# Attention and mixture of experts: early slots on GpSimd, late choices ahead of the shared units, and a reordered opening

## The chip, the cores and the metric

The kernel runs on one core of one Trainium2 chip. The metric is device time in microseconds (us), the median of several runs. The engines are called by their short names: PE is TensorE, DVE is VectorE, ACT is ScalarE, POOL is GpSimd, and SP is SyncE, which here only issues DMAs.

## What is computed

Two batches of 1024 tokens of width 256 go through causal attention with 16 query heads and 4 key-value heads of width 128, with rotary positions, then a layer norm, then a mixture of 64 experts, of which each token takes 6, with two shared units beside them, then a second layer norm. Cut to what matters:

```python
q = q * cos + _rotate_half(q) * sin;  k = k * cos + _rotate_half(k) * sin
attn = softmax(where(causal, q @ k.T * scale, min));  out = (attn @ v) @ Wo.T
x = _layernorm(x + out)
scores = softmax(x @ gate_w.T);  topk_w, topk_ids = top_k(scores, 6)
topk_w = topk_w / (sum(topk_w) + 1e-20)
act = silu(g) * u                       # g, u = x through w_gate_up of each expert, width 176
routed = sum over the 6 experts of topk_w * (act @ w_down.T)
x = _layernorm(x + routed + shared(x))  # shared: the same with ws_gate_up, ws_down, width 352
```

## The kernel before

Every float32 product of the attention and of the experts is made of three products of halves: a value is copied rounded (`..._hi`, on ACT) and the rest is kept (`..._lo`, on DVE or POOL), and PE sums hi*hi, hi*lo and lo*hi (lines 871 to 873).

**Attention** (`attention`, L253) is written as a pipeline over steps. A step scores 128 queries of one head against their keys. There are four rounds of 64 steps (k = 0 to 3), two rounds for each batch, with a part ahead of them (k = -1) that fills the pipeline. In every engine's program the body runs over n from 7 to 70, and each engine does at n what is due for step n, n - 1, n - 2 and so on, in the order in which the lines stand. Semaphores are counted in numbers known when the program is written. What else is due at a step is given by tables. `FILLS` (L82) gives the steps at which PE fills `proj_ps` with the projection of K, of V (T is V's projection, transposed by PE in the fill V), of Q or of the output O; the bank is single, so each fill waits until the one before is copied. `fill_at` (L212) looks the step up, and in the first part puts K at step 51 and T at step 55 by hand. Behind a fill of K or Q comes a turn (rotary position): ACT copies the bank to `taken` (L591), POOL multiplies the two halves of the partitions by the cosine (L528, L530), DVE multiplies by the sine (L784), POOL adds (L538), ACT copies to `q_hi` or `k_hi` (L618), and POOL makes `q_lo` or `k_lo` (L401), except for the first K and the first Q, where DVE does. In the rounds POOL's multiplication is one instruction (L534) for the last turns, and DVE's two (L786, L787).

The first batch's 1024 tokens are routed while the second batch is in attention. `EARLY_DVE` (L91) gives DVE's parts of this by (round, step): statistics, norms, the best 8 of 64 logits, their ids, a mask of the six chosen experts, the softmax weights, and 12 parts "slot" for each of two groups of 512 tokens (L765 to L773): for each of six choices, compare the ids, multiply by `slot_of`, sum over the 64 experts, and convert to an integer address. With such an address POOL sends the tokens' rows to the experts' areas in DRAM (`send`, L492; 48 sends by `EARLY_FILL`), once ACT has filled one of four row buffers. DVE waits behind each slot's operation for its end (`then`).

**The rest** (`feed_forward`, L1045) begins behind a barrier. The other 1024 tokens, in two groups g = 0, 1, are routed by DVE between the units of the shared experts: `tops`, `ids`, `choices`, `masks`, `weights`, `places` and `slot(g, j)`; `notes(g)` puts the weights into the rows, and then POOL may send the rows, 24 indirect DMAs a group (L1272). A shared unit is a gate-and-up product on PE (L1767), a SiLU on ACT (L1362), two products on DVE (`shared_hide`, L1487), a down product on PE (L1781) and an addition on DVE (`shared_add`). When all 48 sends have landed and the last shared unit is gated, SP loads the first expert block's rows (L1209), and a loop over blocks of 256 rows follows, with the expert's weights loaded as they come. At the end the results are summed, normed and stored.

Of the kernel before, what the change touches and what calls it, by code (L numbers as in the profile page):

```python
# [21 lines left out]
F32 = mybir.dt.float32  # L22
# [64 lines left out]
         "O": [4 * (i // 2) + 8 + i % 2 for i in range(2 * QUADS)]}  # L87
ROPES = sorted([("K", i) for i in range(2 * KV_ROUND)] + [("Q", i) for i in range(QUADS)],
# [20 lines left out]
             (2, 43): [(0, "slot", 0)], (2, 47): [(0, "slot", 1)], (2, 50): [(0, "slot", 2)],  # L109
             (2, 51): [(0, "slot", 3), (0, "slot", 4)], (2, 53): [(0, "slot", 5)], (2, 54): [(0, "slot", 6)],  # L110
             (2, 55): [(0, "slot", 7), (0, "slot", 8)], (2, 57): [(0, "slot", 9)], (2, 58): [(0, "slot", 10)],
             (2, 59): [(0, "slot", 11), (1, "norm", 0)], (2, 61): [(1, "norm", 1)], (2, 62): [(1, "norm", 2)],
# [3 lines left out]
             (3, 29): [(1, "weigh", 0)], (3, 30): [(1, "weigh", 1)], (3, 35): [(1, "slot", 0)],  # L116
             (3, 39): [(1, "slot", 1)], (3, 43): [(1, "slot", 2)], (3, 47): [(1, "slot", 3)],
             (3, 50): [(1, "slot", 4)], (3, 51): [(1, "slot", 5), (1, "slot", 6)], (3, 53): [(1, "slot", 7)],
             (3, 54): [(1, "slot", 8)], (3, 55): [(1, "slot", 9), (1, "slot", 10)], (3, 57): [(1, "slot", 11)],
             (3, 58): [(2, "stats", 0), (2, "stats", 1)], (3, 59): [(2, "stats", 2), (2, "stats", 3)],  # L120
             (3, 60): [(2, "moments", 0), (2, "moments", 1)], (3, 62): [(2, "inverse", 0)],
             (3, 63): [(2, "norm", 0), (2, "norm", 1)], (3, 64): [(2, "norm", 2)], (3, 65): [(2, "norm", 3)]}
# [5 lines left out]
BESIDE_COPIED = {(2, 17): (2, 1), (3, 17): (4, 2)}  # L128
RING_ROWS = 4
# [82 lines left out]
def fill_at(n, first):  # L212


    if first and n in (STEPS + FILLS["T"][0], STEPS + FILLS["K"][0]):
        return ("K" if n == STEPS + FILLS["T"][0] else "T"), len(FILLS["K"])
# [36 lines left out]
def attention(nc, dram, resid, consts):  # L253
    with ExitStack() as ctx:
# [34 lines left out]
        stats, moments = sb("early_stats", [P, NORMED, 6]), sb("early_moments", [P, NORMED, 2])  # L289
# [1676 lines left out]
```

## Time and profile before

| | us |
|---|---|
| median of 3 runs | 1334.73 |
| lowest, highest | 1334.47, 1335.14 |
| the profiled execution, whole | 1332.91 |
| its span, from the first instruction to the last | 1331.1 |

Of this span about 28 us are the opening, until the first scores; the four rounds reach to about 905 us; the late tokens' routing and the shared units reach to about 994; the expert loop and the closing take the rest. The profile gives times from the start of the span. A row of the timeline is: start, duration, engine, line of the kernel, operation, what it writes and reads, shapes, and in brackets the idle time of the engine ahead of it with what ended it. A row of instruction groups has, behind the count, the busy time in us and the mean of one in ns, and then the idle time ahead of them. A row of windows has the stretch, its length, the busy times of PE, of PE's weight loads, of DVE, ACT and POOL, each with its number of instructions, then the granted clock of PE as a share of full speed, the share of DMA time and GB/s.

### The profile page before, as it was taken

Reading aid. Unit: us, or ns where it says so; the run is one execution under the profiler, and the core shown is the slowest. Engines: PE = TensorE matmul, PEld = TensorE weight load, DVE = VectorE, ACT = ScalarE, POOL = GpSimd, SP = SyncE. Lnnn points to the kernel's source line nnn. Section 1 sums busy time; section 2 is a strip of 40 time slices with the busy share of each in tenths; the row PEclk is TensorE's granted clock in tenths of the full one; section 3 lists DMA queues with packets and bytes.
Section 4 is the critical chain, followed back from the end, with each engine's and each line's share of the span. In section 5 each row is a group of like instructions: output and inputs, shape, how many; then the busy total and the mean of one; then the engine's idle time right before and its main releaser. Section 6 shows DMA issues by size and latency. Waiting matters only on the chain. (4 is left out here: it accounts for less than half of the span.)

```text
span 1331.1 us, 28521 instructions
## 1 busy us (share of the span) xinstructions
PE 1227.7 (92%) x8636; PEld 1105.6 (83%) x8636; DVE 1023.2 (77%) x2162; ACT 859.0 (65%) x1973; POOL 790.4 (59%) x796
## 2 busy tenths in 40 slices
PE   5899999999999999989999998997969999999967
PEld 3799889889889889878888886886859999999955
DVE  2677777677677777878877887886837999999946
ACT  3665666666576666656666565676227999988932
POOL 5654744654584464365456445443775888888852
PEclk7999999999999999999999999998989999999979
DMA  7766765776558785676577567750357888888857
GB/s 249 204 184 164 187 184 154 186 201 172 147 127 209 212 212 141 164 191 171 162 185 205 136 174 204 187 139 20 95 168 218 259 266 260 255 267 262 263 217 309
DMA packets 196601, 256.51 MB, mean 193 GB/s; under 512 B 13642, under 2 KB 167678, under 8 KB 196500
## 3 DMA queue, kind: packets, MB, share of 16 engines
q1 hardware_dynamic: 183332, 227.85, 61.7%
q0 software_dynamic: 11040, 25.30, 5.7%
q10 hardware_dynamic: 2128, 2.10, 0.5%
q8 instruction: 54, 0.88, 0.3%
q14 instruction: 47, 0.39, 0.1%
HBM read 90.43 MB, written 169.72 MB: 195 GB/s over the span
## 5 line engine op out<-in xcount | busy, mean ns | idle before, releaser
L846 DVE TENSOR_REDUCE neg_max<-scores 128x1 f32<-128x256 f32 (+7 forms) x256 | 192.2, 751 | 152.1 <-PE scores L969 151.4
L608 ACT ACTIVATE pt_hi<-pt 128x512 fp32r<-128x512 f32 (+3 forms) x384 | 174.7, 490 | 188.1 <-PE pt L978 186.1
L581 ACT ACTIVATE probs<-scores,neg_max 128x256 f32<-128x256 f32 (+7 forms) x256 | 189.8, 742 | 48.4 <-DVE neg_max L846 48.3
L802 DVE TENSOR_TENSOR pt_lo<-pt,pt_hi 128x512 fp32r<-128x512 f32 (+3 forms) x384 | 200.3, 549 | 22.7 <-ACT pt_hi L608 21.0
L871 PE MATMUL o_ps<-pt_hi,v_hi 128*128 128x256 f32 (+1 forms) x640 | 193.7, 303 | 8.7 <-DVE o_lo L810 8.5
L872 PE MATMUL o_ps<-pt_lo,v_hi 128*128 128x256 f32 (+1 forms) x640 | 180.0, 281 | 0.0
L873 PE MATMUL o_ps<-pt_hi,v_lo 128*128 128x256 f32 (+1 forms) x640 | 179.6, 281 | 0.0
L978 PE MATMUL pt<-ident,probs 128*128 128x128 f32 x1152 | 169.6, 274 | 6.2 <-DVE pt_lo L802 6.2
L538 POOL TENSOR_TENSOR turned<-turned,turn_sin 128x512 f32<-128x512 f32 x80 | 105.5, 1318 | 114.5 <-DVE turn_sin L784 59.3
L1291 POOL DMA_INDIRECT results_dram<-rows,dest x134 | 145.1, 1083 | 33.1 <-issue 26.4
L969 PE MATMUL scores<-k_hi,q_lo 128*128 128x512 f32 (+4 forms) x384 | 151.8, 395 | 0.0
L528 POOL TENSOR_TENSOR turned<-taken,cos 64x512 f32<-64x512 f32 x60 | 79.5, 1325 | 112.7 <-ACT taken L591 100.2
L978 PEld LDWEIGHTS pt<-ident,probs 128*128 128x128 f32 x1152 | 135.1, 141 | 13.2 <-issue 5.8
L401 POOL TENSOR_TENSOR q_lo<-turned,q_hi 128x512 fp32r<-128x512 f32 x63 | 81.3, 1291 | 101.9 <-ACT q_hi L618 101.3
L964 PE MATMUL scores<-k_hi,q_hi 128*128 128x512 f32 (+4 forms) x384 | 133.2, 347 | 1.6 <-DVE q_lo L401 1.4
L871 PEld LDWEIGHTS o_ps<-pt_hi,v_hi 128*128 128x128 f32 x640 | 121.5, 190 | 14.5 <-issue 7.7
L965 PE MATMUL scores<-k_lo,q_hi 128*128 128x512 f32 (+4 forms) x384 | 131.3, 342 | 0.0
L872 PEld LDWEIGHTS o_ps<-pt_lo,v_hi 128*128 128x128 f32 x640 | 122.2, 191 | 0.0
L873 PEld LDWEIGHTS o_ps<-pt_hi,v_lo 128*128 128x128 f32 x640 | 121.5, 190 | 0.0
L830 DVE SCALAR_TENSOR_TENSOR resid<-proj_ps,row_inv,resid 128x256 f32<-128x256 f32 x256 | 110.0, 470 | 5.9 <-PE proj_ps L873 5.8
L871 PE MATMUL proj_ps<-wo_hi,o_hi 128*128 128x256 f32 x256 | 78.3, 306 | 21.1 <-DVE resid L830 10.4
L871 PE MATMUL proj_ps<-x_hi,w_hi 128*128 128x512 f32 x192 | 79.6, 414 | 15.0 <-DVE w_lo L383 8.0
(280 smaller groups left out, 3680.3 us busy)
## 6 DMA issues: line engine op xcount, KB each, us to landing
rows_dram<-empty SPq DMA_DIRECT2D x256, 524.1 KB
up_raw<-in_up SPq DMA_DIRECT2D x69, 368.0 KB
xt<-rows_dram SPq DMA_DIRECT2D x68, 258.0 KB, 2.7
rows<-results_dram SPq DMA_DIRECT2D x16, 768.0 KB, 12.7
down_raw<-in_down SPq DMA_DIRECT2D x69, 128.0 KB
down_raw<-in_down_tail SPq DMA_DIRECT2D x69, 112.0 KB
w_raw<-in_w SPq DMA_DIRECT2D x8, 768.0 KB, 6.9
wo_raw<-in_wo SPq DMA_DIRECT2D x8, 512.0 KB, 9.5
```

The source lines that it names most:

```text
L581: nc.scalar.activation(probs[:, at_probs(k, m), 0:w], scores_ps[m % 2][:, score_cols(m)], ACT.Exp, bias=neg_max[:, m % 4:m % 4 + 1], accum ...
L608: nc.scalar.activation(pt_hi[m // 2 % 2][:, a:z, P * (m % 2):P * (m % 2) + P], pt_ps[c % 2][:, 0:P * (z - a)].rearrange("p (k q) -> p k q" ...
L802: nc.vector.tensor_tensor(pt_lo[m // 2 % 2][part], pt_ps[c % 2][:, 0:P * (z - a)].rearrange("p (k q) -> p k q", q=P), pt_hi[m // 2 % 2][pa ...
L846: nc.vector.tensor_reduce(neg_max[:, n % 4:n % 4 + 1], scores_ps[n % 2][:, score_cols(n)], AX.X, ALU.max, negate=True).then_inc(max_made, 1)
L871: nc.tensor.matmul(out, lh, rh, start=first, stop=False)
L872: nc.tensor.matmul(out, lh, rl, start=False, stop=False)
L873: return nc.tensor.matmul(out, ll, rh, start=False, stop=last)
L964: nc.tensor.matmul(out, q_hi[b][qt], k_hi[u][:, keys], start=True, stop=False)
L965: nc.tensor.matmul(out, q_hi[b][qt], k_lo[u][:, keys], start=False, stop=False)
L969: mm = nc.tensor.matmul(out, q_lo[b][qt], k_hi[u][:, keys], start=False, stop=True)
L978: mm = nc.tensor.transpose(pt_ps[c % 2][:, (t - a) * P:(t - a + 1) * P], probs[:, at_probs(k, m), t * P:(t + 1) * P], ident[:])
L1291: pool.indirect_dma_start(out=dram["results"], out_offset=bass.IndirectOffsetOnAxis(ap=dest[buf][:, s:s + 1], axis=0), in_=y_sb[buf][:, s, ...
```

## The change

There are four parts.

1. Opening. `OPENING` takes the place of the two steps given by hand: K stays at step 51, T goes from 55 to 53. For the first K and the first Q (`opens`), POOL multiplies only one half of the partitions by the cosine, DVE the other half, and DVE adds (`turn_upper`). The first load of weights is two loads: K's and V's columns, then Q's, with a semaphore of its own (`first_in`) for the first.
2. Early slots. The 24 parts "slot" leave `EARLY_DVE`. `EARLY_SLOT` gives the steps at which POOL makes a slot instead: multiply, six halving additions, and a copy to integers. The six comparisons that DVE makes for the masks are kept in `chosen` for it, partly in the buffer of `x_raw`.
3. Late tokens. In DVE's order `shared_hide(0)` and `tops(1)` go behind `notes(0)`; ACT fills the second rows earlier and makes `exps(0)` ahead of the first SiLU; PE makes `places(0)` ahead of the second unit's product. For this `places(0)` has its results in the second half of the bank `logits_ps[0]` and no longer waits for DVE's first hidden unit, and the first down product waits for `places_taken`.
4. The early statistics buffer is made smaller, with a wait on `moments_made`.

```diff
+OPENING = {STEPS + FILLS["T"][0]: ("K", len(FILLS["K"])), STEPS + FILLS["T"][0] + 2: ("T", len(FILLS["T"])),
+           STEPS + FILLS["K"][0]: None}
...
+EARLY_SLOT = {(2, 48): (0, 0), (2, 50): (0, 1), (2, 52): (0, 2), (2, 54): (0, 3), (2, 56): (0, 4), (2, 58): (0, 5),
+              (3, 34): (1, 0), (3, 46): (1, 1), (3, 50): (1, 2), (3, 52): (1, 3), (3, 54): (1, 4), (3, 58): (1, 5)}
...
+        at_slot = logits
+        chosen_last = x_raw_flat[:, 2 * GT * E:4 * GT * E].bitcast(BF16).rearrange("p (j i e) -> p j i e", j=TOPK - 2, e=E)
+        chosen = [chosen_first[:, j] for j in range(2)] + [chosen_last[:, j] for j in range(TOPK - 2)]
...
-                        sp.dma_start(w_raw[:], dram["w"][bass.ds(kv_at(i), 1)]
+                        cols = slice(0, WCOLS)
+                        if first and i == SPLITS:
+                            sp.dma_start(w_raw[:, :, KV_COLS], dram["w"][bass.ds(kv_at(i), 1), :, :, KV_COLS]
+                                         .rearrange("o p k c -> (o p) k c")).then_inc(first_in, 16)
+                            cols = Q_COLS
+                        sp.dma_start(w_raw[:, :, cols], dram["w"][bass.ds(kv_at(i), 1), :, :, cols]
...
+            def slot(g, j):                        # POOL
+                tiles = slice(GT * g, GT * (g + 1))
+                pool.wait_ge(mask_made, g + 1)
+                pool.wait_ge(slot_of_made, g + 1)
+                pool.wait_ge(weights_made, g + 1)
+                done_steps = E.bit_length() * (g * TOPK + j)
+                pool.tensor_tensor(at_slot, chosen[j], slot_of, ALU.mult).then_inc(slot_step, 1)
+                pool.wait_ge(slot_step, done_steps + 1)
+                for halving in range(E.bit_length() - 1):
+                    some = E >> (halving + 1)
+                    pool.tensor_tensor(at_slot[:, :, 0:some], at_slot[:, :, 0:some], at_slot[:, :, some:2 * some],
+                                       ALU.add).then_inc(slot_step, 1)
+                    pool.wait_ge(slot_step, done_steps + 2 + halving)
+                pool.tensor_copy(slots_int[:, tiles, j], at_slot[:, :, 0]).then_inc(slots_made, 1)
+                pool.wait_ge(slots_made, g * TOPK + j + 1)
...
+                            if opens(first, *use):
+                                made["turn"] += 1
+                                continue
...
                     if k * STEPS + n - 1 in EARLY_FILL:
                         send(EARLY_FILL[k * STEPS + n - 1])
+                    if early_at(EARLY_SLOT, k, n) is not None:
+                        slot(*early_at(EARLY_SLOT, k, n))
...
-                if part == "slot":
-                    j = i // 2
-                    if i % 2 == 0:
-                        then(dve.tensor_tensor(logits, expert_ids[:].unsqueeze(1).broadcast_to([P, GT, E]),
-                                               top_ids[g][:, :, j:j + 1].broadcast_to([P, GT, E]), ALU.is_equal))
-                        then(dve.tensor_tensor(logits, logits, slot_of, ALU.mult))
-                    else:
-                        then(dve.tensor_reduce(slots[:, :, j], logits, AX.X, ALU.add))
-                        dve.tensor_copy(slots_int[:, tiles, j], slots[:, :, j]).then_inc(slots_made, 1)
+            def turn_upper(k, kind, i):            # DVE
+                r = rope_of(kind, i)
+                pos = slice(half(kind, i) * HALF, (half(kind, i) + 1) * HALF)
+                nc.vector.tensor_tensor(turned[r % 2][64:128], taken[r % 2][0:64], cos[0:64, pos], ALU.mult).then_inc(cos_made, 1)
+                dve.wait_ge(cos_made, 2 * now(k, len(ROPES), r + 1))
+                dve.wait_ge(sin_made, now(k, len(ROPES), r + 1))
+                nc.vector.tensor_tensor(turned[r % 2][:], turned[r % 2][:], turn_sin[r % 2][:], ALU.add).then_inc(turn_made, 1)
...
             turn_taken(0)                          # ACT
             fill_rows(0)
+            fill_rows(2)
             turn_taken(6)
             turn_taken(7)
+            exps(0)
             shared_silu_of(0)
-            fill_rows(2)
-            exps(0)
...
             ids(0)                                 # DVE
-            shared_hide(0)
             choices(0)
             masks(0)
-            tops(1)
             weights(0)
             places(0)
             slot(0, 0)
             notes(0)
+            shared_hide(0)
             slot(0, 1)
+            tops(1)
             shared_hide(1)
...
             shared_gate_up(0)                      # PE
             logits(1)
+            places(0)
             shared_gate_up(1)
-            places(0)
```

## Rows read from the trace of the kernel before

**Rows 1.** The page's busy times: engine, us (share of the span), instructions.

```profile
PE 1227.7 (92%) x8636; PEld 1105.6 (83%) x8636; DVE 1023.2 (77%) x2162; ACT 859.0 (65%) x1973; POOL 790.4 (59%) x796
```

**Rows 2.** Timeline, opening: start us, duration, engine, line, operation, [idle before <-releaser].

```profile
7.01 0.69 DVE L383 TENSOR_TENSOR w_lo<-w_raw,w_hi 128x512 fp32r<-128x512 f32 x1 [0.24 <-ACT w_hi L630]
...
14.77 1.26 POOL L538 TENSOR_TENSOR turned<-turned,turn_sin 128x512 f32<-128x512 f32 x1
...
16.66 0.58 ACT L595 ACTIVATE v_turning<-proj_ps 128x512 f32<-128x512 f32 x1
...
17.29 0.50 PE L871 MATMUL proj_ps<-x_hi,w_hi 128*128 128x512 f32 x1 [4.10 <-ACT v_turning L595]
...
22.86 0.80 PE L871 MATMUL proj_ps<-x_hi,w_hi 128*128 128x512 f32 x1 [1.41 <-DVE v_lo L838]
...
27.29 1.57 POOL L528 TENSOR_TENSOR turned<-taken,cos 64x512 f32<-64x512 f32 x1 [1.61 <-DVE q_lo L401]
```

**Rows 3.** Windows, opening: engines' busy times, PEclk, DMA share, GB/s.

```profile
20.00:28.00 8.00, 4.87 (x14) 3.37 (x15) 4.17 (x5) 2.93 (x5) 5.88 (x4) 0.50 0.40 111
```

**Rows 4.** Instruction groups of DVE, 600 to 900 us: the early slots.

```profile
L768 DVE TENSOR_TENSOR x_raw<-expert_ids,early_top_id 128x256 f32<-128x256 f32 x11 | 8.4, 762 | 0.0
...
L772 DVE TENSOR_REDUCE early_slots<-x_raw 128x4 f32<-128x256 f32 x12 | 4.9, 409 | 0.0
L770 DVE TENSOR_TENSOR x_raw<-x_raw 128x256 f32<-128x256 f32 x11 | 4.7, 425 | 0.4
...
L773 DVE CAST early_slots_int<-early_slots 128x4 int32<-128x4 f32 x12 | 3.4, 283 | 0.4
```

**Rows 5.** Instruction groups of POOL, whole span: two widths.

```profile
L401 POOL TENSOR_TENSOR q_lo<-turned,q_hi 128x512 fp32r<-128x512 f32 x63 | 81.3, 1291 | 101.9 <-ACT q_hi L618 101.3 <-DVE early_slots_int L773 0.5
...
L1336 POOL TENSOR_TENSOR resid<-resid,rows 128x256 f32<-128x256 f32 x16 | 11.6, 726 | 26.6 <-DMA rows<-results_dram 26.6
```

**Rows 6.** Windows: the same steps in rounds 2 and 1; a slow clock.

```profile
593.80:637.30 43.50, 43.32 (x291) 39.15 (x292) 36.18 (x74) 27.36 (x64) 23.05 (x17) 0.96 0.66 174
381.80:422.70 40.90, 40.90 (x289) 36.90 (x288) 31.45 (x59) 26.52 (x56) 23.21 (x16) 1.00 0.86 220
...
595.00:598.00 3.00, 3.00 (x16) 2.90 (x16) 1.94 (x4) 1.28 (x4) 0.09 (x1) 0.50 0.79 229
```

**Rows 7.** Timeline at step 44 of round 2; PE's waits, 786:866 (total, times, longest).

```profile
590.20 1.46 DVE L770 TENSOR_TENSOR x_raw<-x_raw 128x256 f32<-128x256 f32 x1
...
592.59 0.35 PE L871 MATMUL o_ps<-pt_hi,v_hi 128*128 128x256 f32 x1 [1.46 <-DVE o_lo L810]
...
PE o_ps L871 <- DVE o_lo L810: 2.4, 3, 1.4
PE pt L978 <- DVE pt_lo L802: 1.5, 2, 1.1
```

**Rows 8.** Timeline of POOL and PE, round 2, ahead of step 52.

```profile
610.14 1.30 POOL L401 TENSOR_TENSOR q_lo<-turned,q_hi 128x512 fp32r<-128x512 f32 x1
...
616.41 0.31 PE L964 MATMUL scores<-k_hi,q_hi 128*128 128x320 f32 x1
```

**Rows 9.** Timeline of DVE, POOL and SP, the late tokens.

```profile
919.07 0.42 DVE L1487 TENSOR_TENSOR shared_hidden<-shared_silu,shared_gate_up 128x256 f32<-128x256 f32 x1 [1.86 <-ACT shared_silu L1363]
...
919.85 2.09 DVE L1538 TENSOR_TENSOR chosen<-expert_ids,top_id 128x256 bf16<-128x256 f32 x6
...
923.71 0.63 DVE L1522 MAX8 top<-logits_ps 128x8 f32<-128x64 f32 x4
...
924.80 0.41 DVE L1551 TENSOR_REDUCE sum_all<-exp_all 128x4 f32<-128x256 f32 x1
...
928.43 1.02 POOL L1272 DMA_INDIRECT rows_dram<-rows,slots_int  x1 [14.23 <-DVE rows L1562]
...
990.15 1.34 POOL L1272 DMA_INDIRECT rows_dram<-rows,slots_int  x1 [0.30 <-issue]
...
993.74 2.89 SPq L1209 DMA_DIRECT2D xt<-rows_dram  x3
```

More of the change, by code:

```diff
@@ L115 @@
              (3, 25): [(1, "mask", 3)], (3, 26): [(1, "mask", 4)], (3, 27): [(1, "mask", 5), (1, "shift", 0)],
[L116 to L122, printed above, removed]
+             (3, 29): [(1, "weigh", 0)], (3, 30): [(1, "weigh", 1)], (3, 58): [(2, "stats", 0), (2, "stats", 1)],
+             (3, 59): [(2, "stats", 2), (2, "stats", 3)], (3, 60): [(2, "moments", 0), (2, "moments", 1)],
+             (3, 62): [(2, "inverse", 0)], (3, 63): [(2, "norm", 0), (2, "norm", 1)], (3, 64): [(2, "norm", 2)],
+             (3, 65): [(2, "norm", 3)]}
 EARLY_DEVIATION = {(1, 60): 0, (2, 20): 1, (3, 61): 2}
@@ L212, in fill_at @@
 def fill_at(n, first):
-    if first and n in (STEPS + FILLS["T"][0], STEPS + FILLS["K"][0]):
-        return ("K" if n == STEPS + FILLS["T"][0] else "T"), len(FILLS["K"])
+    if first and n in OPENING:
+        return OPENING[n]
     for kind, positions in FILLS.items():
@@ L295, in attention @@
         goes_with = sb("early_goes_with", [P, EARLY, WAYS, 2])
-        slots, slots_int = sb("early_slots", [P, GT, TOPK]), sb("early_slots_int", [P, EARLY, TOPK], I32)
+        slots_int = sb("early_slots_int", [P, EARLY, TOPK], I32)
         x_raw_flat = x_raw[:].rearrange("p k t -> p (k t)")
@@ L357, in exchanged, with opens @@
             return k + i // per(kind) < EXCHANGED_ROUNDS
+        def opens(first, kind, i):
+            return first and i == per(kind)
         def turned_into(kind, i):
@@ L507, in body @@
                     if use and use[0] in "KQ" and runs(use[1], per(use[0]), first, last):
-                        if not (first and n < STEPS):
+                        if not opens(first, *use):
                             turn_low(pool, nc.gpsimd, k, *use)
@@ L626, in body @@
                     if runs(i, SPLITS, first, last):
+                        if first and i == SPLITS:
+                            act.wait_ge(first_in, 16)
+                            nc.scalar.activation(w_hi[0][:, :, KV_COLS], w_raw[:, :, KV_COLS], ACT.Copy).then_inc(first_hi_made, 1)
                         act.wait_ge(w_in, 16 * (SPLITS * k + i + 1))
@@ L629, in body @@
                         if first and i == SPLITS:
-                            nc.scalar.activation(w_hi[0][:, :, KV_COLS], w_raw[:, :, KV_COLS], ACT.Copy).then_inc(first_hi_made, 1)
                             nc.scalar.activation(w_hi[0][:, :, Q_COLS], w_raw[:, :, Q_COLS], ACT.Copy).then_inc(w_hi_made, 1)
@@ L743, in route_part @@
                             dve.wait_ge(placed, g)
-                    then(dve.tensor_tensor(picked[:] if i > 0 else mask[:], expert_ids[:].unsqueeze(1).broadcast_to([P, GT, E]),
+                            dve.wait_ge(slots_made, TOPK * g)
+                    then(dve.tensor_tensor(chosen[i], expert_ids[:].unsqueeze(1).broadcast_to([P, GT, E]),
                                            top_ids[g][:, :, i:i + 1].broadcast_to([P, GT, E]), ALU.is_equal))
                     if i > 0:
-                        then(dve.tensor_tensor(mask[:], mask[:], picked[:], ALU.add))
+                        then(dve.tensor_tensor(mask[:], chosen[0] if i == 1 else mask[:], chosen[i], ALU.add))
                     if i == TOPK - 1:
@@ L792, in body @@
                     low = fill_at(n - 3, first)
-                    if first and n < STEPS and low and low[0] in "KQ" and runs(low[1], per(low[0]), first, last):
+                    if low and low[0] in "KQ" and opens(first, *low):
                         turn_low(dve, nc.vector, k, *low)
@@ L814, in body @@
                         turn_by_sine(k, *turn)
+                        if opens(first, *turn):
+                            turn_upper(k, *turn)
                     q = (n - 5) // 4
@@ L1796, in places @@
             def places(g):
-                pe.wait_ge(shared_hidden_made, done(g))
+                if g == 1:
+                    pe.wait_ge(shared_hidden_made, done(1))
                 pe.wait_ge(mask_made, g + 1)
```

32 lines of the change are left out of this document (17 added, 15 removed).

## The prediction

> **What bounds the kernel now.** I read the page's busy times first: TensorE (PE) is busy for 92% of the span and DVE for 77% [rows 1]. So a faster DVE or POOL gains only where PE waits for them, and I looked for such places where the change works. The timeline of the opening gives the first: PE's second projection stands 4.10 us behind ACT's copy `v_turning`, which stands behind POOL's last step of the first turn, from 14.77 to 16.03 us [rows 2]. The second is the stretch of the early slots in rounds 2 and 3. Steps 44 to 56 took 43.5 us in round 2, with 291 matmuls, and 40.9 us in round 1, with 289 [rows 6]; PE waited 1.46 us behind a slot's multiplication [rows 7]. The third is the late tokens: from 928.43 to 990.15 us POOL sends rows without a hole, 48 sends, and only behind the last does SP load the first block's rows, at 993.74 [rows 9]. The shared units run beside these sends, so the start of the first send sets the end. From there the expert loop is untouched, and each microsecond gained ahead of it should reach the end.
>
> **Opening: values two steps ahead.** Fill T moves from step 55 to 53. ACT then copies `v_turning` ahead of `k_hi` instead of behind it. T's matmuls end at 17.29 less the wait of 4.10, or 13.19 us [rows 2]; the copy takes 0.58, and Q0's matmuls start at about 13.85, which is 3.45 us earlier.
>
> **Opening: two loads.** K's and V's weight columns come first. That saves little, since DVE's `w_lo` of these columns started at 7.01 only 0.24 us after `w_hi`, and DVE was busy with `x_lo` up to 6.76. I take 0.25 us (bounds 0 and 0.25; SP has one more issue ahead of the tables, which lie ready long before 11 us). Q0 starts at about 13.6 us.
>
> **Opening: turning by both.** For K0 and Q0 DVE does the second half and the sum. DVE takes 0.69 us for 128x512 (its `w_lo` in [rows 2]) and POOL 1.26 for the sum. Nothing shows how two such operations share SBUF here, except that DVE's slot multiplication took 1.46 us instead of 0.43 beside a POOL operation [rows 4, 7]. So one bound is all in series: 0.69 + 1.26 + 0.69 + 0.69, or 3.4 us with the semaphores; the other is two of them side by side, 2.7 us. By the series bound K0 is turned at 14.7, its split is done by 16.2 (ACT 0.6, DVE 0.69), and Q0, filled from 13.6 to about 15.3, is copied behind `k_hi` by 16.1. Its turn ends at 19.5, `v_lo` at 20.2, and Q1's matmuls start then instead of at 22.86 [rows 2]: 2.6 us earlier, by the other bound 3.4. Q1's copy then no longer waits behind `q_hi`, nor POOL behind DVE's `q_lo` (1.61 us idle ahead of 27.29): 2.9 us for the matmuls, 0.6 for the copy, and POOL begins Q1's turn at 23.9 instead of 27.29. That is 3.4 us in series and 4.2 side by side. PE's granted clock was 0.50 of full in this stretch, the 1.2 GHz level [rows 3]; if PE, with less idle time, keeps 2.4 GHz for Q1's six matmuls, up to 1.3 us come on top. I take 3.8 us, bounds 2.5 and 5.5.
>
> **Slots: what DVE loses.** Twelve slots of 0.76 + 0.43 + 0.41 + 0.28 = 1.88 us [rows 4] leave DVE, 22.6 us in all. Most of it is no gain, since PE did not wait for it. In round 2 the wait of 1.46 us goes [rows 7], and with it probably the drop to half clock behind it (0.50 from 595 to 598 [rows 6], so 1.5 us or more). The excess of 2.6 us over round 1 contains that drop; its other microsecond may belong to the sends, which stay. So round 2 holds between 1.5 and 4.1 us. In round 3 PE waited 2.4 us for `o_lo` and 1.5 for `pt_lo` between 786 and 866 [rows 7]; round 1 has next to nothing of the kind (PE is busy for all of the 40.9 us in rows 6), so I count up to 3.3 us. Together at most 7.4. Masks cost the same number of operations as before (`chosen[0]` takes the place of the first mask).
>
> **Slots: what POOL gets.** POOL's two-input operation takes 0.726 us for 256 columns and 1.291 for 512 [rows 5]: 2.2 ns for a column and 0.16 us fixed. A slot is one of 256 columns (0.73), six additions of 252 columns in all (0.56 + 6 x 0.16 = 1.52) and a copy of 4 (about 0.17): 2.4 us. Eight semaphore waits stand between them; the nearest row is 0.30 us idle between two of POOL's sends [rows 9], and zero is the other end: 2.4 to 4.8 us, and I take 3.2. Behind a slot in POOL's order stand `q_lo`, the turns and the sends, and ACT's `q_hi` waits for the turns. The tightest place is step 48: the slot there stands right ahead of a `q_lo` that ended at 611.44, and PE needed it at 616.41 [rows 8]. That leaves 5.0 - 3.2 = 1.8 us to spare, and 0.2 at the upper bound. Elsewhere a slot fills time in which POOL waited for DVE's sine product. So POOL costs nothing at 3.2 us. New collisions of POOL with DVE's products in SBUF eat something: I take 4.5 us of the 7.4 as the gain of the slots, bounds 1.5 and 7.
>
> **A rule that speaks against it.** The rows show POOL at 1.29 us for what DVE does in 0.69 [rows 2, 5]. The Trainium skill (GPSIMD Engine Reference, Engine selection and Key points) says to leave elementwise work to VectorE, which is about twice as fast, and that both share their SBUF interfaces, with contention when DVE has two SBUF inputs. By that rule a slot costs 3.8 us on POOL and the collisions eat the whole relief; this is the second rival below. Its factor agrees with the trace; that it decides is not shown, since POOL has idle time here and DVE is the engine that PE waits for.
>
> **Late choices ahead of shared units.** In DVE's order the late chain waited 1.86 us for the shared unit's SiLU, did its two products, and began `chosen` at 919.85, though `top_id` was ready when the wait began, at 917.2: 2.65 us. Between the masks and the sums stood `tops(1)`, from 923.71 to 924.80: 1.1 to 1.2 us [rows 9]. Both move behind `notes(0)`, so the first send should start 3.8 us earlier, near 924.6. Is what it needs there? The exponentials: `exps(0)` now comes before the SiLU on ACT, and `weights(0)` begins only near 921, at 924.80 - 3.8. The shifted logits that `exps(0)` takes are ready before `top_id`, at 917, so ACT has 4 us for a table change and two small operations. The places: PE computes them when the masks are ready, near 921.0 (923.71 - 2.65); it needs only the masks and a free bank. `fill_rows(2)` comes earlier on ACT too. PE's second shared unit is held up by 1.6 us for the places, but PE waited later anyway for ACT's copies and for the second masks, which now come 2 us earlier. Later slots are ahead of their sends, four sends of 1.3 us being slower than a slot. The pace from 928.43 to 990.15 over 47 sends, 1.31 us, stays, so the rows are loaded 3.8 us earlier. The bounds are 2.5 (if the places or the table changes are late) and 4.4 (if fewer DVE operations lie beside the sends).
>
> **The sum.** 3.8 + 4.5 + 3.8 = 12.1 us. The profiled execution took 1332.91 us, with a span of 1331.1 and 1.8 us around it; so 1320.8 for an execution like it. The median of the runs is 1334.73, which is 1.8 us more, and so **1322.6 us** for it. All ends together give 1317.8 to 1328.2.
>
> **Rivals.** (1) POOL becomes the bound, and the kernel is slower. For it speaks that in steps 48 to 58 six slots meet POOL's fullest stretch; against it, the idle time that POOL has ahead of its sums. The point from which it decides is a slot of about 5 us, the spare time of step 48. At 7 us a slot, roughly five of the twelve pass 3.6 us on to PE or to ACT's `q_hi`, 18 us, and the slots' own gain stays 4.5: 1334.7 - 7.6 - 4.5 + 18 = 1341 us. (2) Contention eats the slots' gain: DVE's sine products wait beside POOL's new operations as the multiplication did in rows 7, and PE waits as much as before. Then 7.6 us remain: 1327.1 us. (3) The change does not do what it says in the opening: POOL and DVE take turns, PE idles as long as before and runs at half clock, and only 1 us comes of it: about 1325.4. (4) More than the sum: every stall of rounds 2 and 3 goes and the clock never drops: 1317 or less.
>
> **How the numbers follow.** The forecast (1319 to 1326) gets 0.60; the second rival 0.15, the third 0.10, the fourth 0.06. POOL eating all of the slots' gain and part of the rest (1329 to 1337) gets 0.05, and the first rival in full 0.04. The range 1317.5 to 1329 leaves out the first rival and most of the fourth. Within 0.2% (2.7 us) is about what a measurement can't tell from no change; it needs a loss of 9 to 15 us on POOL: 0.04. Slower 0.04, faster 0.92.
>
> **What would show it.** In the opening: `v_turning` ahead of `k_hi` and near 13.3 us, Q0's matmuls at 13.6, PE's first scores near 23. In rounds 2 and 3: POOL's additions at 2.4 to 4.8 us a slot, no PE wait at step 44, no half clock at 595, the stretch of steps 44 to 56 near 41.5 us. Late: first send 3.8 us earlier measured from the late chain's first DVE operation. The prediction is wrong if PE waits for `q_lo` at step 52 of round 2, if ACT waits for POOL's turns, or if the shared units end after the sends.

## The result

The changed kernel took **1325.28 us** as the median of its runs (1324.81 to 1325.92), the kernel before 1334.93 us on the same chip: a ratio of 0.9924, with a 95% interval of 0.9907 to 0.9941. The forecast was 1322.6 us, 12.1 us of gain; about 10 came (7.9 to 12.4 by the interval), and 8.0 between the two profiled executions (spans of 1331.1 and 1323.1 us). The direction and the range held. Two of the three terms came out about as priced. The third, the opening, is worth about 2 us by the medians, half of its price, and nothing by the starts of the steps in the traces.

The busy times of the changed kernel's page stand against [rows 1]: DVE gave 9 us, and POOL took 27 us and 92 instructions. DVE was rid of 21.4 us of slot work [rows 4]; 4.7 us came back as its share of the first two turns, 3.8 us because its sine products (`turn_sin`) took longer, and 3.8 us in `up_lo` of the expert loop (69.9 us instead of 66.0).

```profile
PE 1227.5 (93%) x8636; PEld 1107.3 (84%) x8636; DVE 1014.4 (77%) x2118; ACT 857.2 (65%) x1972; POOL 817.8 (62%) x888
```

**Where the time went.** I took the start of DVE's row maximum of each of the 256 steps (`neg_max`) in both traces and subtracted. First step: 2.1 us earlier than before. Step 8 of round 0 and all the steps from there to step 43 of round 2: 0.6 to 0.8 us *later*. Then 0.8 us earlier at step 44 and 2.9 at the end of round 2; 3.0 at the end of round 3. The first expert block's rows are loaded 7.2 us earlier, and the end comes 8.0 us earlier. So these two executions give: up to step 8 (the opening) +0.7, rounds 2 and 3 (the slots) -3.7, from the last step to the load (the late choices) -4.2, rest -0.8. They are one execution of each kernel, so tenths of a microsecond are not effects of the change by themselves.

**The opening**, as a timeline of the changed kernel, against [rows 2] (columns as there):

```profile
7.38 0.77 PE L910 MATMUL proj_ps<-x_hi,w_hi 128*128 128x512 f32 x1 [7.38 <-DVE w_lo L388]
...
11.96 1.82 POOL L555 TENSOR_TENSOR turned<-taken,cos 64x512 f32<-64x512 f32 x1 [7.53 <-DMA sin<-in_sin]
11.96 0.69 DVE L821 TENSOR_TENSOR turn_sin<-taken,sin 128x512 f32<-128x512 f32 x1 [0.36 <-DMA sin<-in_sin]
...
12.69 1.65 DVE L807 TENSOR_TENSOR turned<-taken,cos 64x512 f32<-64x512 f32 x1
...
13.93 0.60 ACT L627 ACTIVATE v_turning<-proj_ps 128x512 f32<-128x512 f32 x1 [3.02 <-PE proj_ps L912]
...
14.58 0.79 PE L910 MATMUL proj_ps<-x_hi,w_hi 128*128 128x512 f32 x1 [0.69 <-ACT v_turning L627]
...
15.16 0.63 ACT L650 ACTIVATE k_hi<-turned 128x512 fp32r<-128x512 f32 x1 [0.63 <-DVE turned L810]
15.17 0.63 PE L911 MATMUL proj_ps<-x_lo,w_hi 128*128 128x512 f32 x1
...
15.60 0.63 PE L912 MATMUL proj_ps<-x_hi,w_lo 128*128 128x512 f32 x1
...
17.54 0.60 ACT L623 ACTIVATE taken<-proj_ps 128x512 f32<-128x512 f32 x1 [1.75 <-PE proj_ps L912]
...
21.92 0.80 PE L910 MATMUL proj_ps<-x_hi,w_hi 128*128 128x512 f32 x1 [2.61 <-DVE v_lo L877]
```

The order is the one foretold: `v_turning` ahead of `k_hi`, PE's wait of 4.10 us down to 0.69. But look at the starts of the matmuls at 15.17 and 15.60: 0.43 us apart, which is 512 columns at 1.2 GHz. In the kernel before, the matmuls of V's projection lay 0.23 us apart. The changed kernel's PE keeps this spacing, the half clock, from its first matmul to 24.2 us; the records of the granted clock begin only at 25.4. Then it is at full clock, and then at half again in the dense steps behind, from 32.2 to 39.1 us (columns as in [rows 6]):

```profile
32.20:39.10 6.90, 6.27 (x24) 5.19 (x23) 3.89 (x8) 3.67 (x11) 4.18 (x3) 0.51 0.68 179
```

**The slots.** Groups of POOL, 575 to 905 us; then the windows from step 44's row maximum to step 56's and of the old slow stretch, which answer to [rows 6]; then PE's waits from 786 to 866 us, against [rows 7]:

```profile
L521 POOL TENSOR_TENSOR x_raw<-x_raw 128x256 f32<-128x256 bf16 x8 | 5.5, 691 | 0.1
L525 POOL TENSOR_TENSOR x_raw<-x_raw 128x128 f32<-128x128 f32 x12 | 5.5, 460 | 0.9
...
L525 POOL TENSOR_TENSOR x_raw<-x_raw 128x4 f32<-128x4 f32 x12 | 2.5, 205 | 0.9
```

```profile
593.10:635.70 42.60, 42.26 (x292) 37.83 (x293) 32.32 (x57) 27.22 (x64) 34.47 (x50) 1.00 0.70 183
595.00:598.00 3.00, 2.78 (x23) 2.37 (x22) 2.56 (x7) 2.09 (x6) 1.32 (x2) 1.00 0.90 219
```

```profile
PE proj_ps L910 <- DVE resid L869: 2.8, 2, 2.0
PE o_ps L910 <- DVE o_lo L847: 2.3, 2, 1.7
PE proj_ps L910 <- DVE v_lo L877: 1.5, 1, 1.5
PE pt L1017 <- DVE pt_lo L839: 0.5, 1, 0.5
```

The stretch runs at full clock and takes 42.6 us, where 41.5 was forecast and 43.4 was measured before. By the same two row maxima it takes 39.7 us in round 1 (375.3 to 415.0); the window of round 1 in [rows 6] holds steps 47 to 58, so the excess of round 2 was 3.7 us and not 2.6, and 2.9 of it are still there. Round 2 gains 1.4 us at step 44, 1.1 more up to step 47, loses 0.4 up to step 56, and gains 1.4 from there to its end. In round 3 the waits for `pt_lo` fell from 1.5 to 0.5 us, those for `o_lo` are as long as before. One of these is new, and it comes from a slot. The timeline shows how POOL's slot at step 34 of round 3 pushes back the turn, ACT's `q_hi`, the `o_lo` of DVE and with it PE:

```profile
794.01 0.69 POOL L521 TENSOR_TENSOR x_raw<-early_chosen,x_raw 128x256 f32<-128x256 bf16 x1
794.79 2.75 POOL L525 TENSOR_TENSOR x_raw<-x_raw 128x128 f32<-128x128 f32 x6
...
799.29 1.28 POOL L568 TENSOR_TENSOR turned<-turned,turn_sin 128x512 f32<-128x512 f32 x1
800.66 0.63 ACT L650 ACTIVATE q_hi<-turned 128x512 fp32r<-128x512 f32 x1 [1.40 <-POOL turned L568]
...
802.17 0.36 PE L910 MATMUL o_ps<-pt_hi,v_hi 128*128 128x256 f32 x1 [1.72 <-DVE o_lo L847]
```

**The late tokens**, against [rows 9]: timelines of DVE, POOL and SP. The late chain's first operation is the first line here; before, it stood at 908.81.

```profile
905.86 1.41 DVE L1539 BATCH_NORM_STATS2 late_stats<-resid 128x6 f32<-128x256 f32 x4 [3.55 <-PEq L252]
...
914.29 2.10 DVE L1577 TENSOR_TENSOR chosen<-expert_ids,top_id 128x256 bf16<-128x256 f32 x6
...
918.18 0.42 DVE L1590 TENSOR_REDUCE sum_all<-exp_all 128x4 f32<-128x256 f32 x1 [0.15 <-DVE mask L1584]
...
921.93 1.20 POOL L1311 DMA_INDIRECT rows_dram<-rows,slots_int  x1 [10.67 <-DVE rows L1601]
...
986.58 2.89 SPq L1248 DMA_DIRECT2D xt<-rows_dram  x3
```

### The profile page after: what moved, and what is told of

Read it like the earlier page. It is cut to its first block and busy times, and to the rows that moved or that the text cites. A ratio compares the mean times of both kernels' runs of the same rounds, so it can differ in the third digit from the quotient of the medians.

```text
span 1323.1 us, 28589 instructions
## 1 busy us (share of the span) xinstructions
PE 1227.5 (93%) x8636; PEld 1107.3 (84%) x8636; DVE 1014.4 (77%) x2118; ACT 857.2 (65%) x1972; POOL 817.8 (62%) x888
## 5 line engine op out<-in xcount | busy, mean ns | idle before, releaser
L568 POOL TENSOR_TENSOR turned<-turned,turn_sin 128x512 f32<-128x512 f32 x78 | 102.0, 1307 | 92.4 <-DVE turn_sin L821 53.4
L555 POOL TENSOR_TENSOR turned<-taken,cos 64x512 f32<-64x512 f32 x60 | 80.0, 1334 | 110.7 <-ACT taken L623 99.3
```

## Experiments: does each part give what it was priced at?

The first three kernels do one part of the change each, on the kernel before; the fourth does slots and late choices without the opening. Their diffs are parts of the change's own: `OPENING`, the two loads, `opens` and `turn_upper` in e1; `EARLY_SLOT`, `slot` on POOL, `chosen` and the smaller statistics buffer in e2; the two orders of the late tokens and `places_ps` in e3.

**e1, the opening alone.** 

> The kernel before with the opening of the change alone (T at step 53, turning by POOL and DVE, two loads). Theory A (the clock): the first scores come 2.5 us earlier, as in the change, but the half-clock stretch then falls into the first dense steps instead of into the waits ahead of them, and from step 4 of round 0 on the kernel is 0.7 us later than before: ratio 1.000 to 1.001. Theory B (the opening works and its gain was lost by something in the slots or the late part): 2 to 4 us faster, ratio 0.997 to 0.9985.

Measured: 1332.48 us, ratio 0.9987 (0.9977 to 0.9996), 0.5 to 3.1 us faster. That lies between the two theories. By the steps theory A holds: the half stretch stands at 33.1 to 40.0 us, and step 8 is 1.4 us later than in the kernel before and stays so to the end of round 3. This execution is 2.5 us faster in the rest, behind the last step, where the opening changes nothing.

**e2, the slots alone.** 

> The kernel before with the early slots on POOL alone. Theory A (the parts add up, each as the comparison of the traces reads it): rounds 2 and 3 give 3.7 us, so 3 to 4.5 us faster, ratio near 0.9972. Theory C (the gain of the slots is mostly the half-clock stretch at 595 us that is gone, an accident of where the clock looks): the gain depends on what stands ahead, so 1 to 6 us.

Measured: 1330.27 us, ratio 0.9970 (0.9961 to 0.9979), as theory A has it; theory C's range of 1 to 6 us holds it too.

**e3, the late choices alone.** 

> The kernel before with the late choices moved alone. Theory A: the first send starts 3.6 us earlier and the rows load 4.2 us earlier; 4 to 5 us faster, ratio near 0.9966. Rival: the shared units or the expert loop's first weights end last instead, and less than 2.5 us reach the end.

Measured: 1329.36 us, ratio 0.9964 (0.9950 to 0.9978), as theory A has it.

**e4, everything but the opening.** 

> The change without its opening (slots and late choices kept). Theory A: 0.7 us faster than the change, so 8.5 to 10.5 us faster than before, ratio near 0.993. Theory B: 2 us or more slower than the change, ratio 0.994 to 0.996.

Measured: 1325.61 us, ratio 0.9938 (0.9925 to 0.9952), between the two theories; it does not decide between them.

The parts add up: 0.9987 x 0.9970 x 0.9964 = 0.9921, and the whole change has 0.9924. In microseconds of 1334.6 these are 1.7, 4.0 and 4.8, with intervals of 0.5 to 3.1, 2.8 to 5.2 and 2.9 to 6.7. Between e4 (0.9938) and the change (0.9924) lie 1.9 us, with intervals that overlap. So by the medians the opening gives about 2 us, not 3.8, and is the term that failed; by the starts of the steps it gives none. The record does not resolve this difference: the profiled execution of the kernel before was 1.6 us faster than the median of 20 runs, and which of its stretches were fast is not known.

The traces of e1 to e4 show the other two terms in finer steps. For the slots, the steps gain 3.5 us (e2, from +0.5 to -3.0) and 3.5 (e4, from -0.1 to -3.6) in round 2, 2.5 of it between steps 43 and 47: the wait itself, then the clock. A part of that is luck, as one theory had it: e3, whose slots are on DVE as before, had the PE wait at step 44 but no half clock behind it, gained 1.2 us there, and lost 2.1 between steps 42 and 46 of round 3, where it had two half stretches (815.9 to 819.3 and 826.1 to 829.5 us) that the kernel before has not. For the late choices, the time from the last step's maximum to the load of the first rows is 103.4, 102.5 and 103.8 us in the three kernels without them (before, e1, e2) and 99.2, 99.2 and 99.3 in those with them (change, e3, e4): 3.2 to 4.5 us less. The steadiest part of it is the start of the first send, counted from the late chain's first operation: 19.62 to 19.64 us in the first three, 16.06 or 16.07 in the other three. What remains behind that load varies from 335.8 to 337.4 us among these kernels without any pattern, so the change's "rest -0.8" can't be told from no effect.

## Experiments: where the opening's gain went

**e6, work for PE in the gaps.** The changed kernel with 36 matmuls whose results nobody reads, 12 of them ahead of the first projection:

```
+            def keep_busy(count):
+                for _ in range(count):
+                    nc.tensor.matmul(o_ps[:, 0:P], ident[:], ident[:], start=True, stop=True)
+            keep_busy(12)
...
                 for n in range(FIRST, FIRST + STEPS):
+                    if first:
+                        keep_busy({55: 0, 56: 2, 59: 2, 61: 8, 66: 4, 67: 8}.get(n, 0))
```

> The changed kernel, with some matmuls added that compute nothing: 12 of 128x128 at the start of PE's order and 24 more in five gaps of the opening, into a bank that is free then. Theory A (the opening's gain is lost to the granted clock: half from 32.2 to 39.1 us, in dense steps): if PE's added work moves or removes the half stretch, the loss of 3.4 us goes, so the steps from round 0 step 8 on start 2 to 3.4 us earlier and the median is 1322 to 1323.5. Theory B (the opening's gain is lost to the queue behind q_hi and POOL's sum, the gap of 1.91 us at 29.4): the clock may change but the offset of +0.7 us at step 8 stays, 1325.3. If the fill work delays real work instead: up to 1 us slower.

Measured: 1318.57 us, ratio 0.9873 (0.9859 to 0.9887), 6.7 us below the change's median. That is twice what theory A said. The steps from step 8 on are 6.6 to 7.2 us earlier than in the change, but for seven of round 3 (5.1 to 5.8). PE ran at full clock from its first projection; no half stretch until 690 us. Its timeline:

```profile
10.39 1.83 POOL L555 TENSOR_TENSOR turned<-taken,cos 64x512 f32<-64x512 f32 x1 [5.95 <-DMA sin<-in_sin]
...
11.11 1.66 DVE L807 TENSOR_TENSOR turned<-taken,cos 64x512 f32<-64x512 f32 x1
...
12.53 0.50 PE L917 MATMUL proj_ps<-x_hi,w_hi 128*128 128x512 f32 x1 [0.24 <-ACT v_turning L627]
...
12.86 0.40 PE L918 MATMUL proj_ps<-x_lo,w_hi 128*128 128x512 f32 x1
...
13.10 0.39 PE L919 MATMUL proj_ps<-x_hi,w_lo 128*128 128x512 f32 x1
...
18.61 0.51 PE L917 MATMUL proj_ps<-x_hi,w_hi 128*128 128x512 f32 x1 [1.29 <-DVE v_lo L877]
...
20.34 0.33 PE L1012 MATMUL scores<-k_hi,q_hi 128*128 128x128 f32 x1
```

The starts at 12.86 and 13.10 are 0.24 us apart, and the first scores stand at 20.34 instead of 24.64. The tables, too, were usable at 10.39 us here and at 11.96 in the change, but that is not where the change lost. In the five kernels with the new opening and no added work (change, e1, e5, e7, e8) the first scores come 17.26 or 17.27 us after the first matmul, while POOL's first multiplication starts anywhere from 11.52 to 12.07 us; the row at 17.54 above shows ACT waiting for PE there, not for a turn. So PE's half clock sets the first scores of these kernels. In e6 they come 12.47 us after the first matmul, 4.8 us less. Only at full clock do the tables set them: in e6, e11 and e12 the first scores come 9.94 to 9.96 us after POOL's first multiplication, which starts at 10.39, 11.19 and 10.79 us.

**e9, the same added work with the old opening.** 

> Slots and late choices changed, opening as before (as in e4), with the same 36 matmuls that compute nothing as in e6. It asks what the opening's edits are worth when the clock is held. Theory A (the edits gain about 2.5 us up to the first scores, as the trace of the change shows, and the clock's half stretch took it back): 2.5 to 3.5 us slower than e6, about 1321.5. Rival B (the edits gain nothing, and e6's gain of 6.8 us is that of the added matmuls alone): the same as e6, 1318.6, within 0.8 us.

This kernel and e10, e11 and e12 ran on a chip on which the kernel before took 1378.0 us; the late sends and the rest are slower there, while the attention steps are not, so I compare their steps and leave the medians at ratios. Measured: ratio 0.9950 (0.9921 to 0.9979), against 0.9908 (0.9872 to 0.9945) for e11, which has the new opening and one slot moved; the intervals overlap, so the steps have to speak. Step 8 is 5.8 us later than in e6, hardly earlier than in the kernel before (6.0 later than e6). The added work alone gives 0.2 us at step 8. The old order still makes PE wait for 3.65 us, from 12.84 to 16.49, and the clock falls in that wait, at 15.4:

```profile
16.49 0.79 PE L906 MATMUL proj_ps<-x_hi,w_hi 128*128 128x512 f32 x1 [3.65 <-ACT v_turning L618]
17.08 0.63 PE L907 MATMUL proj_ps<-x_lo,w_hi 128*128 128x512 f32 x1
17.51 0.63 PE L908 MATMUL proj_ps<-x_hi,w_lo 128*128 128x512 f32 x1
```

Neither theory named this outcome in full: by the steps the edits gain 5.8 us if PE is kept busy, more than the 2.5 to 3.5 expected, and next to nothing if it is not.

**e10, POOL turning alone again, with the added work.**

```
-                            if opens(first, *use):
-                                made["turn"] += 1
-                                continue
...
-                        if opens(first, *turn):
-                            turn_upper(k, *turn)
```

> e6 with the first K's and Q's turn done by POOL alone again; values still two steps ahead, first weights in two loads. It prices DVE's half of the turn. By the prediction's series bound DVE saves 0.6 us for the half and 0.6 for the sum, twice over: 2.4 us less 0.7 for the extra wait, so e6 + 1.2 to 2.4 us if PE waits for both turns; by the trace of the change, where DVE's half (1.65 us) stood beside POOL's operation (1.82 us), it saves about 0.6 us a turn: e6 + 0.6 to 1.2 us. Rival (DVE was needed for its own splits): e6 or less.

Measured: ratio 0.9905 (0.9873 to 0.9937), too wide for the median to speak. Step 8 is 2.2 us later than in e6, the upper end of the first estimate. From POOL's first multiplication to `k_hi` it took 4.64 us (10.29 to 14.93), in e6 3.20; PE waited 3.14 us for `q_lo` ahead of the first scores, with a half stretch from 23.1 us behind it.

**e7, one load for the first weights.**

```
-                        if first and i == SPLITS:
-                            sp.dma_start(w_raw[:, :, KV_COLS], ...).then_inc(first_in, 16)
-                            cols = Q_COLS
```

> The changed kernel, with the first weights in one load again, everything else changed. In the changed kernel the K and V columns land 1.0 us earlier, but the Q columns' copy (ACT L665) starts at 9.29 instead of 6.89 us and the tables land at 11.96 instead of 11.53. Theory A (the second load pays back what the first gains): the tables land 0.3 to 0.4 us earlier, the first turn ends as early, the first scores within 0.3 us, 1325.3 or less. Theory of the prediction: one load costs 0.25 us; by the first matmul (7.96 against 7.38) 0.6 us. All three within 0.6 us of 1325.3.

Measured: 1323.46 us, ratio 0.9908 (0.9892 to 0.9923), single runs from 1318.9 to 1326.1. The median is 1.8 us below 1325.3, where all three theories had 0.6 at most; the two intervals overlap. The tables landed 2.8 us earlier (9.05 us instead of 11.84), and that brought nothing, as said above: the first scores came 17.27 us after the first matmul, as in the change. What the second load can give is an earlier first matmul. It came at 8.16 us here and at 7.38 to 7.96 in the four kernels with two loads and no added work; but the five kernels with the old opening, all with one load, have 7.72 to 8.30, and those with two loads and added work 7.61 to 8.20. So 0.6 us of one pair of traces is no more than the spread. From step 8 on e7 was 0.2 us ahead of the change, with a half stretch of 3.4 us instead of 6.8. At the end nothing of the second load can be seen, and its sign stays open.

**What the traces of the opening say together.** From the first maximum to that of step 8 it took 18.8 or 18.9 us in the four kernels with the old opening and no added work. With the new opening: 21.7 to 22.0 us in three kernels with a half stretch of 6.8 us (change, e1, e5), 20.1 and 20.7 with one of 3.4 us (e8, e7), and 19.5 in those with none (e6, e11, e12). So the half stretch of 6.8 us costs 2.3 us in these steps. The other 0.7 us (19.5 against 18.8) has no run of its own; I read it as the queue behind POOL's turn of Q1, but e9, with the old opening, has 19.3, so it is not shown. The new opening brings the first maximum about 2 us forward (26.1 to 26.9 us against 28.1 to 29.0) and pays it back by step 8.

## Experiments: slots, places and prices

**e5, one slot moved.**

```
-              (3, 34): (1, 0), (3, 46): (1, 1), ...
+              (3, 38): (1, 0), (3, 46): (1, 1), ...
```

> The changed kernel, with one slot moved: tile group 1's first slot goes from step 34 of round 3, where it stood ahead of POOL's turn and sum (L564, L568) and ran from 794.01 to 797.79 us, to step 38, where POOL was idle from 802.64 to 805.28. Theory A (slots on POOL are free only where POOL is idle): the PE gap of 1.72 us ahead of step 38 and ACT's wait of 1.40 us for the turn's sum go, and nothing takes their place, since POOL's own next sum waits for DVE until 808.6 anyway: 0.8 us faster by the steps' offsets (-2.8 before it, -2.0 behind), up to 2.5 us if the half clock from 813.9 to 817.3 goes too. About 1324. Rival (the gap comes from the exchange of round 3's other load, wo_hi, on ACT): gap and clock stay, 1325.3.

Measured: 1322.25 us, ratio 0.9897 (0.9882 to 0.9911). The slot stands where POOL was idle, and POOL waits for DVE instead of the reverse; the window below is that of the change's half stretch from 813.9 to 817.3, which is gone:

```profile
797.56 1.29 POOL L568 TENSOR_TENSOR turned<-turned,turn_sin 128x512 f32<-128x512 f32 x1 [1.63 <-DVE turn_sin L824]
...
801.70 0.69 POOL L521 TENSOR_TENSOR x_raw<-early_chosen,x_raw 128x256 f32<-128x256 bf16 x1
802.47 2.05 POOL L525 TENSOR_TENSOR x_raw<-x_raw 128x128 f32<-128x128 f32 x6
...
812.00:818.00 6.00, 6.00 (x44) 5.24 (x44) 3.77 (x9) 4.39 (x15) 5.21 (x5) 1.00 0.91 191
```

By the steps it gained 1.5 us up to step 38 and 3.0 up to step 48, and kept 1.7 at the round's end (the median is 3.0 us below the change's, where theory A had 2.5 at most, with intervals that just overlap), since a wait of 1.74 us for `o_lo` appeared at step 52. e11 shows the same: -1.5, -3.0, -2.0. The rival falls.

**e8, a slot of twice the length.** The multiplication is done five times over, which changes no result:

```
+                for again in range(5):
+                    pool.tensor_tensor(at_slot, chosen[j], slot_of, ALU.mult).then_inc(slot_step, 1)
+                    pool.wait_ge(slot_step, done_steps + 1)
```

> The changed kernel, with each slot's multiplication on POOL done five times instead of once: a slot takes 3.15 + 4 x 0.77 = 6.2 us instead of 3.15. The first rival of the prediction puts the point from which POOL decides at 5 us a slot (1.8 us to spare at step 52 of round 2 behind a slot of 3.2). Theory A (that point is right): PE waits 1.2 us for q_lo at step 52, and the slots of steps 50 to 58 and 46 to 58 each pass on one to three us, so 8 to 15 us slower than the change, 1333 to 1340. Rival (POOL has more slack, since its sum waits for DVE behind nearly every turn): under 5 us slower, below 1330.

Measured: 1352.95 us, ratio 1.0141 (1.0126 to 1.0156): 27.7 us above the change, about twice the upper end of the theory's 8 to 15, and slower than the kernel before. Timeline of POOL, then the waits of 600 to 665 us (total, times, longest):

```profile
607.26 3.73 POOL L522 TENSOR_TENSOR x_raw<-early_chosen,x_raw 128x256 f32<-128x256 bf16 x5
611.07 2.05 POOL L528 TENSOR_TENSOR x_raw<-x_raw 128x128 f32<-128x128 f32 x6
613.19 0.19 POOL L531 CAST early_slots_int<-x_raw 128x4 int32<-128x4 f32 x1
613.46 1.76 POOL L406 TENSOR_TENSOR q_lo<-turned,q_hi 128x512 fp32r<-128x512 f32 x1
```

```profile
ACT pt_hi L643 <- PE pt L1020: 12.2, 10, 2.5
DVE o_lo L850 <- ACT o_hi L607: 9.7, 4, 5.2
ACT q_hi L653 <- POOL turned L571: 8.7, 2, 4.8
PE o_ps L913 <- DVE o_lo L850: 6.2, 2, 3.7
PE scores L1006 <- POOL q_lo L406: 1.9, 2, 1.6
```

A slot takes 6.1 us (7.2 at most). PE waits 1.6 us for `q_lo` at step 52, as computed (1.2). The larger price is the path that the prediction only listed as a sign of failure: ACT stands 4.8 us in one piece behind POOL's turn, and everything queued behind `q_hi` on ACT (`o_hi`, `pt_hi`) stands with it. The twelve slots together took 76.9 us instead of 38.5; of these 38 us more, 27.7 reached the end.

**e11, both findings.** 

> The changed kernel with both findings: group 1's first slot at step 38 (e5) and the added matmuls in the opening (e6). If the two gains add up: 6.7 + 1.0 to 3.0 us below the change's 1325.3, so 1315.6 to 1317.6. If e6 already has what e5 gained (in its profiled run the steps from 28 on of round 3 were 0.5 us earlier still): 1318.5.

Measured: ratio 0.9908 (0.9872 to 0.9945) on the slower chip. By the steps the added work gave what it gave in e6 (0.8 us less, with a first multiplication of POOL 0.8 us later) and the moved slot 2.0 us at the end of round 3. So the gains add up in the attention part; the median, with an interval of 10 us, can't confirm it, and the best kernel with a measured median is e6.

**e12, work for PE ahead of the expert blocks.** e11 with this behind the last shared unit:

```
+            for _ in range(24):
+                nc.tensor.matmul(gate_up_ps[1][:, 0:P], ident[:], ident[:], start=True, stop=True)
             pe.wait_ge(shared_added, done(UNITS // 2 - 1))
```

> e11 with 24 more matmuls that compute nothing, in the 6.8 us in which PE waits for the first expert block's rows (from 981.8 us on); half clock stood behind that wait for 10.2 us in every run so far (984.5 to 994.8 in the change). Theory A (PE's idle time brings the drop, and PE's pace is the limit right behind it): the half stretch goes or shortens and the end comes 1 to 3 us earlier than e11. Rival (the start of the expert loop goes at DVE's and the loads' pace): the clock rises and the end stays, within 0.7 us of e11.

Measured: ratio 0.9916 (0.9886 to 0.9946). On this chip there was almost no gap to fill: in e11 PE idled 1.75 us ahead of the first block, where the change on the faster chip has 6.79. The added work takes 5.5 us (each added matmul stands as two records). The expectation's "10.2 us in every run so far" was not so either: the kernel before and e2 have 13.7. Timeline of PE, and the windows from 1010 to 1030 us of e12 and, below, of e11:

```profile
1015.07 5.52 PE L1927 MATMUL shared_gate_up<-ident 128*128 128x128 f32 x48
1020.42 0.60 PE L1891 MATMUL first_tail_ps<-ident,xt 128*128 128x128 f32 x4
...
1010.00:1030.00 20.00, 17.52 (x131) 16.46 (x129) 9.47 (x21) 8.63 (x17) 5.33 (x13) 1.00 0.47 134
```

```profile
1010.00:1030.00 20.00, 15.36 (x85) 13.84 (x84) 9.35 (x21) 8.63 (x17) 5.33 (x13) 0.83 0.53 148
```

The clock stayed full, and the added work held up the first block by 2.65 us (1020.42 against 1017.77 in e11). From that block to the end it took 343.4 us, in e11 343.0: the higher clock bought nothing that can be seen (from the rows' load to the end the four kernels on this chip take 349.1 to 353.3 us), which speaks for the rival. What it would give on a chip that has the gap wasn't tried.

## Why the prediction was right, and where not

**Opening (-3.8; measured -1.7 alone, about -2 within the change).** The mechanism was right and its size was not. *The order* came as told. *Turning by both*: the series bound said 3.4 us with the semaphores, and to the start of `k_hi`, from 11.96 to 15.16, it took 3.20. *Two loads*: the first matmul came 0.58 us earlier, more than the 0.25 taken, but no more than the spread (e7); and "the tables lie ready long before 11 us" was wrong. The two weight loads put the issue of `sin` at 3.25 us instead of 2.19, and both engines waited for it until 11.96. At PE's half clock that wait cost the first scores nothing. *The clock* is the step that failed. I took PE's pace from rows at full clock and saw the half clock only as a possible extra gain for Q1 ("up to 1.3 us on top"). In fact the matmuls of V and Q0 ran at 0.43 us each instead of 0.23, which makes Q0 start at 14.58 instead of 13.6 and Q1 at 21.92 instead of 20.2. The full clock was luck of the execution that I read: with the same old opening V's matmuls ran at 0.23 us in the kernel before and e4, and at 0.43 in e2 and e3, where the first scores came 19.8 us after the first matmul instead of 19.2 or 19.3. The half stretch, at 18.0 to 31.7 us before, where PE had idle time anyway, now came at 32.2 to 39.1, in dense steps, and took 2.3 us there. With PE kept busy (e6) both losses went, and the first scores came at 20.34 instead of 24.64. The third rival had this result (1325.4 us, "only 1 us comes of it") with half of its reason: DVE and POOL did take turns and PE did run at half clock, but it did not idle as long as before.

**Slots (-4.5; measured -4.0 alone).** A slot takes 3.1 us on POOL (3.4 to 3.8 for three of the twelve), where I took 3.2. Spare time at step 52 was enough; there was no PE wait of 1.46 us at step 44 and no half clock at 595. But the half clock at 595 is absent in e3 as well, with the slots still on DVE, so that part of the gain may be luck. The stretch of steps 44 to 56 took 42.6 us and not 41.5: the comparison with round 1 was read from other steps. What I missed is the first slot of round 3, which I had counted among those that fill idle time: its place was looked at for `q_lo` and not for the turn. It costs 1.5 us directly, up to 3 with the clock, and 1.7 by the round's end (e5). The second rival, contention, is there but did not decide: from 580 to 905 us DVE's 46 sine products took 41.1 us instead of 37.5 (40.6 in e2, 37.5 in e1 and e3, which have no slots on POOL), yet PE's waits shrank from 4.0 to 3.4 us between 575 and 640 and from 8.8 to 7.1 between 786 and 866. The rest of the gain goes with the half stretch at 595 that is absent.

The rows had POOL at nearly twice DVE's time for an operation. The rule of the Trainium skill (GPSIMD Engine Reference, Engine selection) to leave elementwise work to VectorE did not decide at 3.1 us a slot and did at 6.1 (e8). I had put the point at 5 us, which lies between; the price behind it was too low: 18 us for 7 us a slot, against 27.7 measured for 6.1. I had counted five slots passing on their excess, once each, and not what is queued behind `q_hi` on ACT.

**Late choices (-3.8; measured -4.8 alone, -4.2 from the trace before to that of the change).** The first send starts 16.07 us behind the chain's first operation, before 19.62: 3.55 us. With these edits it is 3.2 to 3.6 us less in every trace, against the 3.8 of the forecast. The other 0.66 us come in the 48 sends, 64.65 instead of 65.31 us from the first to the rows' load; e1, which has none of the late edits, took 64.29, so they are not shown to be the change's. The places and the exponentials were there in time: DVE waited 0.15 us ahead of the sums.

## What to carry over

Price a shortened wait with the clock that PE will have, read from more than one execution, and look at where the half stretch goes when the gaps ahead of it move: a gain at the head of a dense stretch can be paid back inside it. Where PE must wait, cheap matmuls in the gap can be worth more than the edit itself, but only once the gap is short enough to fill. When work moves to another engine, check each place of it for every consumer of that engine, and for what is queued behind that consumer.

## What the runs showed of the hardware

Operations with two SBUF inputs each, one on POOL and one on DVE, ran nearly one behind the other. In e6 POOL's 64x512 began at 10.39 together with DVE's sine product. The product took 0.69 us, as it does alone (0.68), and POOL's operation 1.83 us, ending at 12.22; alone it takes 1.26 (L530 at 13.44 us of the kernel before). DVE's own 64x512 then took 1.66 us, where DVE's 64x512 products alone take 0.69 (L786), and ended at 12.77, 0.55 us behind POOL. All three together took 2.38 us; their times alone add up to 2.63. The Trainium skill (SBUF — State Buffer, SBUF: two separate sides) describes this as an exclusive lock that is held for a whole instruction; the trace agrees in the main, with 0.25 us less than a strict series of the times alone.

The same tables, issued at 3.25 us, landed between 10.2 and 11.9 us in the eight kernels with two loads. No trace here shows the cause of that spread of 1.8 us. It reached the first scores only where PE was kept at full clock.
